# Four attention layers on one core: row maxima formed for two batches at once with GpSimd, weights three batches behind, norms moved to ScalarE

## The chip, the cores and the metric

The kernel runs on one core of a Trainium2 chip. The metric is the device time of one execution in microseconds. An engine is named as in the profile: PE (TensorE, its weight loads are PEld), DVE (VectorE), ACT (ScalarE), POOL (GpSimd), SP (SyncE, here only an issuer of DMAs).

## What is computed

A residual stream `x` of 32 batches x 128 tokens x 128 features goes through four pairs of a gated attention and a gated feed-forward part. Cut to what matters here:

```python
x = x + tanh(g_xattn[0]) * attn0(x, ctx)     # 16 heads of 8, keys from the context, masked
x = x + tanh(g_ffn[0])   * ffn0(x)           # dense, ternary weights, 128 -> 512 -> 512 -> 512 -> 128
x = x + tanh(g_xattn[1]) * attn1(x, ctx)     # 16 heads of 8, keys from the context and from x
u = mla_attention(norm(x))                   # causal, 16 heads of 4; then 8 experts, the best 2
x = x + tanh(g_ffn[1])   * (u + experts1)
x = x + tanh(g_xattn[2]) * attn2(x, ctx)     # 8 heads of 16, masked
x = x + tanh(g_ffn[2])   * (norm(x) + experts2)
x = x + tanh(g_xattn[3]) * depool(x, ctx)
x = x + tanh(g_ffn[3])   * quantised_ffn(x)  # int8-like activations: round(v * 127 / max|v|), clipped
```

Each attention is `softmax(q k^T) v` over 128 queries and 128 or 256 keys.

## The kernel before, in words

**A planner and five programs.** `make_plan` (line 491) writes out by hand one list of steps. `reckon` (line 97) gives each kind of step its cost per engine in nanoseconds and `LANDING` the time of its DMAs; `Plan.do` keeps a clock for each engine with them. Work that is not in the main loop (norms, transposes, splits, loads, expert blocks) waits in the list `side` and is put between main steps by `run_side`, `fill` and `flush`, as the planner's clocks say that its inputs are there. Then `tensor_program`, `vector_program`, `scalar_program`, `pool_program` and `sync_program` walk the same list, and each issues what is its own. So every engine's queue is in order, all waits are semaphore counts, and a cost in `reckon` changes no instruction but can change the order of all of them.

**An attention** (`attention`, line 730) works on batches in 32 time steps plus a `lag`. In step t it makes the scores of batch t (`s_unit`) and the weights of batch t - lag (`st_unit`). Scores are queries x keys into PSUM on PE; DVE reduces them over the keys to negated row maxima `mneg` (`scores`, line 2052). The weights need the transposed scores (keys x queries) less the maximum: PE computes them again the other way round over 99 rows instead of 96, where rows 96 to 98 of the tile `Q8` hold the maximum in three bf16 parts, and ACT takes the exponential out of PSUM (line 2428). PE then multiplies them with the values (`sums`).

**The maxima's way** (`max_parts`, `m_turn`): when the last scores of a batch are reduced, DVE makes the three bf16 parts with four small instructions (lines 2061 to 2064), PE transposes them (line 1722), ACT copies them to `mT` (line 2419), and SP stores them into `Q8` with three DMAs, for each batch. `lag` is 2 for 16 heads and 4 for 8 heads. The weights of a batch wait for these DMAs (`maxima`).

**Rows of the heads.** Queries and keys are split into bf16 parts (`split`, on POOL or DVE), stored to scratch memory in HBM (`parts_store`, three DMAs for a destination) and loaded back in the layout of the heads (`rows_load`: 384 KB a tile for 8-wide heads). Tiles hold three pairs of batches. The loads of pair p are issued at the end of time step `load_step[p] = max(2 * (p - A.R) + 1 + lag, 2 * p - 4)`, where `A.R` is 3 for 16 heads, and its scores start in step 2p.

**Norms**: DVE takes the statistics (`norm_in`, lines 2003 and 2006), POOL the reciprocal root (lines 2642 to 2659), DVE writes the result (`norm_out`, lines 2025 to 2029). **Experts**: blocks of 256 sorted tokens; for the first experts ACT does the tanh, DVE the gate (lines 2257, 2259) and the copy of the output out of PSUM (`block_down`, line 2265). POOL scatters the tokens (line 2622) and fetches the results (line 2628) with indirect DMAs. **The quantised part**: DVE scales and rounds in two instructions (2357, 2358: adding a large constant rounds) and clips, ACT takes the constant off (2539); for the hidden layer ACT scales (2551), DVE rounds and clips (2380), POOL takes the constant off (2677).

The stages by time in the profile: first attention 43 to 330 us, dense part 330 to 631, second attention 631 to 987, causal attention with the expert front beside it 987 to 1367, rest of the first blocks to 1535, third attention with blocks and fetches 1535 to 1790, second experts, depool and quantised part 1790 to 2425.

## Time and profile before

| | |
|---|---|
| median of 3 runs | 2424.68 us (2423.02 to 2434.64) |
| the profiled execution | 2426.92 us |
| its span, first to last instruction | 2425.1 us |
| PE busy | 1735.3 us, 72% |
| DVE busy | 1436.1 us, 59% |
| ACT busy | 918.9 us, 38% |
| POOL busy | 702.1 us, 29% |
| mean granted TensorE clock | 0.811 |

The span is the trace's; the 1.8 us around it belong to the execution. The engines' busy times overlap, and none fills the span, so the table alone does not name a bound; the waits inside a stage do. In the timeline a number in brackets is the idle time of the engine ahead of the instruction and what ended it.

### The profile page before, as it was taken

What the parts mean: (1) busy time and instruction counts of PE and PEld (TensorE: products, weight loads), DVE (VectorE), ACT (ScalarE), POOL (GpSimd) and SP (SyncE); (2) the same over time, 40 slices, a digit from 0 to 9 for tenths busy, and PEclk for the clock granted to TensorE, in tenths of its full rate; (3) what the DMA queues carried; (4) which work ended last, traced back from release to release, by engine and by line L of the source; (5) the groups of instructions that cost most, each with busy time, mean ns of one, the idle gap of its engine ahead of it and who ended that gap; (6) DMA issues with size and microseconds to landing.
All of it is one profiled execution on the core that took longest, in us unless ns stands there. A gap on an engine that the chain in (4) does not pass through costs nothing. (4 is left out here: it accounts for less than half of the span.)

```text
span 2425.1 us, 42255 instructions
## 1 busy us (share of the span) xinstructions
PE 1735.3 (72%) x14902; PEld 1225.0 (51%) x14902; DVE 1436.1 (59%) x4230; ACT 918.9 (38%) x1768; POOL 702.1 (29%) x1027
## 2 busy tenths in 40 slices
PE   2667879999688898898888875664661497874423
PEld 1344447677476666554545663553341486763212
DVE  5566655543476766567666556554774523648666
ACT  2334443333155555443333432231330264653223
POOL 3322100100331222124433116215426402151653
PEclk9878779999788888899888896796675698986555
DMA  6535546300155554321221112634520222120100
GB/s 174 117 82 107 113 125 213 70 1 1 35 98 94 107 94 78 97 48 48 55 50 48 43 64 63 138 95 140 116 63 29 77 71 66 58 68 22 42 27 9
DMA packets 189756, 184.46 MB, mean 76 GB/s; under 512 B 29508, under 2 KB 177924, under 8 KB 183556
## 3 DMA queue, kind: packets, MB, share of 16 engines
q1 hardware_dynamic: 180540, 145.04, 25.8%
q10 hardware_dynamic: 816, 19.92, 2.7%
q0 software_dynamic: 8192, 16.79, 2.4%
q8 instruction: 122, 2.00, 0.4%
q14 instruction: 86, 0.70, 0.1%
HBM read 119.47 MB, written 80.74 MB: 83 GB/s over the span
## 5 line engine op out<-in xcount | busy, mean ns | idle before, releaser
L2052 DVE TENSOR_REDUCE mneg<-psb 128x4 f32<-128x512 f32 (+1 forms) x576 | 387.5, 684 | 207.6 <-PE psb L1671 173.2
L2428 ACT ACTIVATE HB<-psb 128x512 f32<-128x512 f32 x384 | 222.3, 596 | 253.2 <-PE psb L1671 234.6
L1671 PE MATMUL psb<-K,Q 96*128 96x128 bf16 x1280 | 189.3, 251 | 54.0 <-DMA Q<-sc_q 32.1
L1671 PE MATMUL psb<-Q,K 99*128 99x128 bf16 x1280 | 147.9, 247 | 110.1 <-DMA Q<-mT 108.4
L2428 ACT ACTIVATE HB<-psb,bias 128x512 f32<-128x512 f32 x192 | 131.7, 686 | 227.5 <-PE psb L1671 201.7
L2646 POOL TENSOR_SCALAR rs<-mv 128x2 f32<-128x2 f32 (+1 forms) x96 | 22.3, 232 | 658.2 <-DVE mv L2006 650.3
L1671 PEld LDWEIGHTS psb<-Q,K 99*128 99x128 bf16 x1280 | 110.4, 113 | 146.0 <-issue 131.2
L1671 PEld LDWEIGHTS psb<-K,Q 96*128 96x128 bf16 x1280 | 112.1, 111 | 112.0 <-issue 54.0
L1671 PE MATMUL psb<-HB,VA 128*9 128x128 f32 (+1 forms) x2560 | 148.7, 311 | 27.3 <-ACT OE L2433 27.0
L1671 PE MATMUL psb<-K 128*128 128x256 f32 x576 | 155.6, 417 | 3.4 <-issue 1.5
L1671 PE MATMUL psb<-KS,Q 96*128 96x128 bf16 x1024 | 151.1, 238 | 9.2 <-DVE mneg L2052 8.3
L1671 PEld LDWEIGHTS psb<-K 128*128 128x128 f32 x576 | 114.2, 209 | 22.6 <-issue 6.1
L1671 PE MATMUL psb<-HB,VS 128*9 128x128 f32 (+1 forms) x2048 | 111.2, 293 | 2.3 <-issue 2.3
L1671 PE MATMUL psb<-Q,KS 99*128 99x128 bf16 x1024 | 109.5, 234 | 3.3 <-DMA Q<-mT 3.2
L1671 PE MATMUL psb<-cnegb,identb 128*128 128x512 bf16 x256 | 109.2, 427 | 0.5 <-issue 0.5
L1671 PEld LDWEIGHTS psb<-KS,Q 96*128 96x128 bf16 x1024 | 91.8, 106 | 27.8 <-DVE mneg L2052 12.0
L1671 PE MATMUL psb<-WB,HB 128*128 x768 | 98.2, 281 | 9.8 <-issue 7.4
L1683 PE MATMUL psb<-cst,OE 128*128 128x128 f32 x480 | 95.4, 325 | 13.4 <-issue 5.8
L1671 PEld LDWEIGHTS psb<-WB,HB 128*128 128x128 f32 x768 | 97.2, 198 | 13.1 <-issue 10.3
L2270 DVE TENSOR_TENSOR K<-psb,HB 128x256 f32<-128x256 f32 x48 | 20.4, 425 | 137.9 <-PE psb L1671 105.4
L1671 PE MATMUL psb<-biasT,selbb 96*128 96x512 bf16 x192 | 92.7, 483 | 1.0 <-issue 1.0
L1671 PEld LDWEIGHTS psb<-Q,KS 99*128 99x128 bf16 x1024 | 78.6, 105 | 23.2 <-issue 11.0
(433 smaller groups left out, 4031.8 us busy)
## 6 DMA issues: line engine op xcount, KB each, us to landing
tok_rows<-in_zero ACTq DMA_DIRECT2D x16, 1152.0 KB, 30.9
K<-sc_k SPq DMA_DIRECT2D x32, 384.0 KB, 4.9
Q<-sc_q SPq DMA_DIRECT2D x32, 384.0 KB
sc_q<-comp SPq DMA_DIRECT2D x48, 192.0 KB
K<-tok_rows SPq DMA_DIRECT2D x72, 128.0 KB
y_rows<-K SPq DMA_DIRECT2D x72, 128.0 KB
sc_q<-comp SPq DMA_DIRECT2D x48, 128.0 KB
vraw<-in_ctx SPq DMA_DIRECT2D x48, 128.0 KB, 7.0
```

Source lines behind the costliest of these rows:

```text
L1671: return pe.e.matmul(out, w, x, start=start, stop=stop, skip_group_check=True)
L1683: t = pe.e.transpose(o[:, 128 * j:128 * j + 128], src[:, 128 * j:128 * j + 128], ident)
L2052: t = e.tensor_reduce(m.mneg[:, s.b % 4, s.i * A.per:(s.i + 1) * A.per], PSB[s.use.bank].rearrange("p (h k) -> p h k", h=A.per), AX.X, ALU ...
L2270: v.done(e.tensor_tensor(y2, o2, m.b2bc[:, bass.ds(at_, 128)].unsqueeze(1).broadcast_to([128, 2, 128]), ALU.add), s.use.drained)
L2428: a.done(act(m.HB[:, s.slot, :], PSB[s.use.bank], ACT.Exp, bias=bz), s.use.drained)
L2646: then(e.tensor_scalar(r0, var, EPS, None, ALU.add))
```

## The change

- **Maxima.** DVE's four instructions a batch go. Once for two batches PE transposes `mneg` in fp32 (two instructions, into 16 or 8 rows x 256), ACT copies the result twice (to `m32` in fp32, to `mT` in bf16), POOL makes the second and third part with three instructions, and SP stores both batches with three DMAs (`max_store`).
- **Lag.** `lag` for 16 heads is 3 instead of 2. By the formula of `load_step` the row loads of pair p are then issued at the end of step 2p - 2 instead of 2p - 3. The weights of both batches of a pair wait for the one store.
- **Norms.** In the four attentions `norm_out` of the queries' input is ACT's (scale and bias); POOL makes the bias -mean * rstd with two instructions more, except in the causal attention, where the input is scaled only.
- **First experts.** `block_down` with its factor 2 is ACT's.
- **Rounding.** `quant_in` multiplies and adds the constant in four instructions of 128 columns; `quant_int` is POOL's and clips; the hidden layer's scaling by ACT goes, DVE scales and rounds in one, POOL clips and takes off the constant.
- **Planner.** The costs of SP's steps go from 100 to 250 up to 350 to 1500 for a destination or load; new kinds get costs. A copy of the values may be placed earlier (`copied`).
- **Constants.** Three constant blocks used only at the start lie in `U`, so the constants come in two DMAs.

```diff
-        self.lag = 2 if H == 16 else 4
+        self.lag = 3 if H == 16 else 4
...
-        "parts_store": lambda: (("sp", 250 * len(s.dests)),),
-        "rows_load": lambda: (("sp", 100),),
+        "parts_store": lambda: (("sp", 1500 * len(s.dests)),),
+        "rows_load": lambda: (("sp", 1100 if A.dh == 16 else 600),),
...
-        "max_parts": lambda: (("dve", 1050),),
-        "max_rows": lambda: (("pe", 130), ("act", 290), ("sp", 250)),
+        "max_rows": lambda: (("pe", 240), ("act", 760), ("pool", 2000)),
+        "max_store": lambda: (("sp", 1800),),
...
-            if i == n_s - 1:
-                k = b % 4
-                flush(("m", b - 4))
-                t = inc("dve", "max_parts")
-                do("max_parts", A=A, b=b, k=k, need=u.drained, free=mcb_free[k], done=t)
-                soon(lambda: m_turn(b, t), t, 0, ("m", b), m_turn)
+            if i == n_s - 1 and b % 2:
+                soon(lambda: m_turn(p, u.drained), u.drained, 0, ("m", p), m_turn)
+        def m_turn(p, t):
+            flush(("m", p - 1))
+            u = use(misc(), "act")
+            parts = inc("pool", "max_parts")
+            do("max_rows", A=A, p=p, need=t, use=u, free=(m32_free[0], mT_free[p % 2]), cst=t_cst, done=parts)
+            mneg_free[p % 2] = u.full
+            m32_free[0] = parts
+            soon(lambda: m_store(p, parts), parts, 0, ("m", p), m_store)
+        def m_store(p, parts):
+            do("max_store", A=A, p=p, need=parts, rows=prepped[p]["qk"])
+            mT_free[p % 2] = ready_m[p] = dma(f"dma_m{p % 2}", 3)
...
+        for b2 in range(2):
+            t = pe.e.transpose(PSB[s.use.bank][0:s.A.H, 128 * b2:128 * b2 + 128], m.mneg[:, 2 * (s.p % 2) + b2, 0:s.A.H], C("ident"))
...
+        act(m.m32[0:H, :], PSB[s.use.bank][0:H, 0:256], ACT.Copy)
+        a.done(act(m.mT[0:H, s.p % 2, 0, :], PSB[s.use.bank][0:H, 0:256], ACT.Copy), s.use.drained)
...
+        x, parts = m.m32[0:H, :], m.mT[0:H, s.p % 2]
+        g.wait_ge(before[0], s.use.drained)
+        step(e.tensor_tensor(x, x, parts[:, 0, :], ALU.subtract))
+        g.wait_ge(before[0])
+        step(e.tensor_copy(parts[:, 1, :], x))
+        g.wait_ge(before[0])
+        done(e.tensor_tensor(parts[:, 2, :], x, parts[:, 1, :], ALU.subtract), s.done)
...
+            then(e.tensor_tensor(mean, mean, r1, ALU.mult))
+            done(e.tensor_scalar(mean, mean, -1.0, None, ALU.mult), s.rstd)
...
-        v.wait_ge(v.step(e.tensor_tensor(b4(xf), b4(xf), Sc[:, :, 0:1].broadcast_to([128, 4, 128]), ALU.mult)))
-        v.done(e.tensor_scalar(xf, xf, MAGIC, MAGIC + 127.0, ALU.add, ALU.min), s.done)
+        for j in range(4):
+            t = e.tensor_scalar(b4(xf)[:, j, :], b4(xf)[:, j, :], Sc[:, j, 0:1], MAGIC, ALU.mult, ALU.add)
+        v.done(t, s.done)
...
-        v.done(e.tensor_scalar(m.H[s.k][s.j], m.H[s.k][s.j], MAGIC, MAGIC + 127.0, ALU.add, ALU.min), s.rounded)
+        v.done(e.tensor_scalar(m.H[s.k][s.j], m.H[s.k][s.j], m.sc[:, s.k, s.j, 4:5], MAGIC, ALU.mult, ALU.add), s.rounded)
...
+        done(e.tensor_scalar(m.qn[s.k], m.xf3[s.k], MAGIC + 127.0, -MAGIC, ALU.min, ALU.add), s.done)
```

## Rows read from the trace of the kernel before

**Rows 1.** Windows by stage: busy us (x instructions) of each engine, PEclk, DMA share, GB/s.
```profile
core 0: us, PE busy (x) PEld busy (x) DVE busy (x) ACT busy (x) POOL busy (x), PEclk, DMA share, GB/s
43.00:330.00 287.00, 207.27 (x2273) 124.55 (x2270) 183.15 (x495) 109.03 (x198) 58.03 (x87) 0.82 0.46 93
...
631.00:987.00 356.00, 297.62 (x4255) 229.50 (x4254) 246.53 (x606) 188.97 (x392) 94.81 (x168) 0.84 0.48 89
987.00:1367.00 380.00, 324.83 (x3088) 197.65 (x3084) 242.36 (x816) 145.24 (x316) 123.03 (x220) 0.87 0.21 56
...
1535.00:1790.00 255.00, 171.67 (x1393) 120.29 (x1393) 161.99 (x525) 82.49 (x174) 89.69 (x140) 0.74 0.47 117
1790.00:2425.00 635.00, 338.57 (x2105) 268.71 (x2105) 358.21 (x1189) 225.66 (x447) 231.83 (x286) 0.70 0.15 45
```

**Rows 2.** Who waited for mT (us, times): first, second, causal attention, in this order.
```profile
  PE psb L1671: 64.1, 15
...
  PE psb L1671: 41.2, 13
...
  PE psb L1671: 4.5, 3
```

**Rows 3.** Timeline, one pair of batches in the first attention: start, us, engine, instruction [idle].
```profile
193.76 1.53 SPq L2687 DMA_DIRECT2D sc_k<-comp  x3
...
196.62 0.32 SPq L2687 DMA_DIRECT2D K<-sc_k  x1
196.86 0.26 ACT L2419 ACTIVATE mT<-psb 48x128 bf16<-48x128 bf16 x1
...
197.92 1.77 SPq L2687 DMA_DIRECT2D Q<-mT  x3
...
200.58 0.31 DVE L2061 CAST mcb<-mneg 128x16 bf16<-128x16 f32 x1
...
205.53 0.58 PE L1671 MATMUL psb<-Q,K 99*128 99x128 bf16 x4 [4.60 <-DMA Q<-mT]
...
219.52 0.31 DVE L2061 CAST mcb<-mneg 128x16 bf16<-128x16 f32 x1
```

**Rows 4.** Windows inside that pair, columns as in rows 1.
```profile
206.00:213.00 7.00, 7.00 (x62) 4.17 (x64) 3.22 (x9) 2.82 (x5) 0.00 (x0) 0.51 0.38 107
```

**Rows 5.** Timeline, second attention: row loads, the store of maxima behind them, PE's wait.
```profile
766.84 0.33 SPq L2687 DMA_DIRECT2D K<-sc_k  x1
...
769.77 1.79 SPq L2687 DMA_DIRECT2D Q<-mT  x3
...
778.25 0.38 PE L1671 MATMUL psb<-Q,K 99*128 99x128 bf16 x4 [2.61 <-DMA Q<-mT]
```

**Rows 6.** Timeline of POOL in the causal attention: first and last of 8 scatters.
```profile
1201.05 1.12 POOL L2622 DMA_INDIRECT tok_rows<-HB,pidx  x1 [0.19 <-issue]
...
1210.05 0.96 POOL L2622 DMA_INDIRECT tok_rows<-HB,pidx  x1 [0.30 <-issue]
```

**Rows 7.** Timeline, first attention: the first of five POOL clears, a cast of DVE beside them.
```profile
110.70 3.51 POOL L2578 MEMSET KS<- 96x4096 bf16 x1
...
118.18 3.32 DVE L2063 CAST mcb<-mres 128x16 bf16<-128x16 f32 x1
```

**Rows 8.** Windows of the tile mcb alone, summed over the four attentions.
```profile
sum 1278.00, PE 32.18 PEld 12.97 DVE 109.47; mean PE 8.05 PEld 3.24 DVE 27.37
```

**Rows 9.** Groups by line and form: out<-in xcount | busy us, mean ns | idle before, releaser.
```profile
L2673 POOL TENSOR_TENSOR comp<-r,comp 128x256 bf16<-128x256 f32 x80 | 54.5, 681 | 6.4
...
L2677 POOL TENSOR_SCALAR Q<-Q 128x512 bf16<-128x512 f32 x16 | 24.2, 1512 | 8.4 <-DVE Q L2380 7.2
...
L2029 DVE TENSOR_SCALAR xn<-X,mv,rs 128x128 f32<-128x128 f32 x96 | 32.5, 408 | 4.4 <-POOL rs L2648 4.2
L1683 PE MATMUL psb<-cst,xn 128*128 128x128 f32 x128 | 32.1, 340 | 39.4 <-DVE xn L2029 28.9 <-issue 10.0 <-ACT mT L2419 0.5
...
L2551 ACT ACTIVATE Q<-Q,sc 128x512 f32<-128x512 f32 x32 | 20.5, 711 | 14.7 <-DVE sc L2374 14.7
...
L2414 ACT ACTIVATE xT<-psb 128x256 f32<-128x256 f32 x48 | 18.2, 382 | 59.6 <-PE psb L1683 52.7 <-remote 6.8
```

More of the change, by code:

```diff
@@ L157, in reckon @@
         "block_gate": lambda: (("dve", 1400),),
-        "block_down": lambda: (("pe", 900 if s.i == 0 else 1800), ("dve", 450)),
+        "block_down": lambda: (("pe", 900 if s.i == 0 else 1800), ("act", 480) if s.i == 0 else ("dve", 450)),
         "fetch": lambda: (("pool", 2550),),
@@ L458, in C @@
         o, w = CST[name]
-        return self.cst[:, o:o + w]
+        if o < CST["cneg"][0]:
+            return self.cst[:, o:o + w]
+        o -= CST["cneg"][0]
+        return self.U[:, :, :].rearrange("p b d -> p (b d)")[:, o:o + w]
     def col(self, name, i=0):
@@ L673, in norm_in, with norm_out @@
         return s
[L675 to L677 removed]
+    def norm_out(s, dst, free=None, done="normed", second=None, by="dve"):
+        t = inc(by, f"{done}_{by}")
+        do("norm_out", norm=s, dst=dst, free=free, done=t, second=second, by=by)
         return t
@@ L1946, in run_program, with norm_source, norm_views @@
             part(s)
+def norm_source(m, what, j):
+    name, i = what
+    if name in ("X", "U"):
+        return (m.X if name == "X" else m.U)[:, i + j, :]
+    if name == "CX":
+        return m.CX[:, j, 0:128]
+    return b4(m.xf3[i])[:, j, :]
+def norm_views(m, s, j):
+    name, i = s.dst
+    src = norm_source(m, s.second[0] if s.second else s.norm.src, j)
+    o = slice(128 * j, 128 * j + 128)
+    if name == "xn_heads":
+        return m.xn[:, i, o].rearrange("p (d h) -> p h d", h=16), src.rearrange("p (h d) -> p h d", h=16)
+    if name == "U":
+        return m.U[:, i + j, :], src
+    return (m.xn[:, i, o] if name == "xn" else m.nf[:, o] if name == "nf" else m.xf3[i][:, o] if name == "xf3"
+            else m.UP[:, o] if name == "UP" else x_front(m, s.dst)[:, o]), src
 def vector_program(v, plan, m, cu):
@@ L1989, in setup @@
             t = v.done(e.tensor_copy(m.biasT[:, i, :], PSB[7].bitcast(BF16)[0:96, 128 * i:128 * i + 128]), u.drained)
-    def source(what, j):
-        name, i = what
-        if name in ("X", "U"):
-            return (m.X if name == "X" else m.U)[:, i + j, :]
-        if name == "CX":
-            return m.CX[:, j, 0:128]
-        return b4(m.xf3[i])[:, j, :]
     def norm_in(s):
@@ L2009, in norm_out @@
     def norm_out(s):
-        nm, (name, i) = s.norm, s.dst
+        if s.by != "dve":
+            return
+        nm = s.norm
         v.wait_ge(nm.rstd, s.free)
@@ L2408, in setup, with norm_out @@
             a.done(t, ("clear_act", i + 1))
+    def norm_out(s):
+        if s.by != "act":
+            return
+        nm = s.norm
+        a.wait_ge(nm.rstd, s.free)
+        if s.second:
+            a.wait_ge(s.second[1])
+        for j in range(nm.n):
+            dst, src = norm_views(m, s, j)
+            if s.second:
+                t = act(dst, src, ACT.Copy, scale=m.rs[:, nm.k, j, 0:1])
+            else:
+                t = act(dst, src, ACT.Identity, bias=m.mv[:, nm.k, j, 0:1], scale=m.rs[:, nm.k, j, 1:2])
+        a.done(t, s.done)
     def transpose_x(s):
@@ L2515, in block_up, with block_down @@
             a.done(t, u.drained)
+    def block_down(s):
+        if s.i == 0:
+            a.wait_ge(s.use.full, s.free)
+            a.done(act(m.buf[0][s.h].ys[s.j % 3], PSB[s.use.bank][:, 0:256], ACT.Copy, scale=2.0), s.use.drained)
     def k8_ones(s):
@@ L2647, in norm_in @@
         if not s.twice:
-            done(e.tensor_tensor(r1, r0, power, ALU.pow), s.rstd)
+            if s.by == "act":
+                then(e.tensor_tensor(r1, r0, power, ALU.pow))
+                shift()
+            else:
+                done(e.tensor_tensor(r1, r0, power, ALU.pow), s.rstd)
             return
@@ L2697, in cst_load @@
     def cst_load(s):
-        load("cst", m.cst[:, :], io["cst"])
+        n, w = CST["cneg"][0], sum(w for _, w in CST.values())
+        load("cst", m.cst[:, :], io["cst"][:, 0:n])
+        load("cst", m.U[:, :, :].rearrange("p b d -> p (b d)")[:, 0:w - n], io["cst"][:, n:w])
     def ints_load(s):
```

171 lines of the change are left out of this document (74 added, 97 removed).

## The prediction

> **What bounds the kernel now.** I began with the windows by stage [rows 1]. PE is busy for 72%, 84% and 85% of the first, second and causal attention, at a granted clock of 0.82 to 0.87; behind 1790 us no engine is over 57%, so that stage is a chain of latencies. A busy PE at a low clock is not a PE at its peak, so I asked who waits. In the trace of the tile `mT` PE waits 64.1 us in the first attention, 41.2 us in the second and only 4.5 us in the causal one [rows 2]. The timeline of one pair shows the kind of wait [rows 3]: ACT has the maxima at 197.12 us, SP is just issuing row loads, stores at 197.92 to 199.69, and PE goes on at 205.53, 5.8 us after the last store was issued and after 4.60 us idle. The second attention repeats it: row loads from 766.84, the store at 769.77 to 771.56, PE idle for 2.61 us to 778.25 [rows 5]. Each costs twice: in the 7.0 us behind the wait PE is busy 7.00 us at a granted clock of 0.51, its lower level (1.2 of 2.4 GHz) [rows 4]. At the upper one this would be some 3.6 us, so 3.4 us more are lost. The pair takes 219.52 - 200.58 = 18.9 us; without wait and low clock it would be 18.9 - 4.6 - 3.4 = 10.9 us, some 5.5 us a batch.
>
> **The change, part by part.**
>
> **Maxima, first attention.** Removed: DVE's four instructions a batch, 109.5 us in all four attentions, 0.86 us a batch [rows 8]. DVE is busy for 64% there [rows 1] and PE sets the pace, so this buys nothing by itself. The new chain, from the last reduction of a pair: two fp32 transposes, no dearer than the 0.34 us of a full one [rows 9], 0.7 us; two ACT copies at 0.38, 0.8; three POOL instructions at most at 0.68, 2.0; three DMA issues 1.8 [rows 3]; landing. The landing is bounded by 1.3 us (a key store's last issue ends at 195.29, the load that waits for it goes at 196.62) and 5.8 us (behind row loads) [rows 3]. I take 2, near the first, because the store is now planned about 4.5 us into a step and the row loads at its end, so it goes ahead of them. With some 0.8 us (my estimate) for finishing what ACT, PE and POOL have in hand the chain is 8.1 us (7.4 to 11.9). It is covered by one batch: both batches of a pair wait for one store, and the first is due one whole step after the last reduction, as before. In the first attention 5.5 us cover it, so 2.6 us of wait stay in each pair, with a low clock behind about half of them, 1.7 us. The stage's mean pair is 287 / 16 = 17.9 us [rows 1], the new one 10.9 + 2.6 + 1.7 = 15.2, plus 1 us for row loads (below): 16.2 us, and 16 x 1.7 = 27 us are won. The five POOL clears at 110.7 to 126.2 us [rows 7] stand in the maxima's way once, some 7 us. **-20 us** (-70 to +20).
>
> **Lag and row loads.** They now have one step to land instead of two. From 766.84 to 778.25, 11.4 us, everything issued there had landed, maxima last [rows 5]; the rows alone must be earlier. The second attention's step without wait would be 356 / 32 - (2.6 + 3.4) / 2 = 8.1 us [rows 1, 4, 5]. So I allow 1 us a pair in both attentions; the ends are 0 and 3.3 us, 11.4 less 8.1.
>
> **Maxima, second attention.** The chain of 8.1 us meets a cover of 8.1 us: the wait goes. A pair is now 22.3 us, then 16.3 + 1 = 17.3, and 5 us a pair would be won. For a quarter of the pairs I keep the low clock, 0.9 us, and I add 1.2 us for the extra instructions of PE and ACT in front of their matmuls (two fp32 transposes and a norm on ACT, 0.34 to 0.4 us each [rows 9]). That leaves 2.9 us, x 16 = **-47 us** (-90 to 0).
>
> **Causal attention.** Almost no wait for maxima stands there [rows 2], so none can be won. DVE loses 0.86 us and half a norm of 2 x 0.41 us a batch [rows 8, 9], about 1.3 x 32 = 40 us of 242 busy [rows 1]; with PE busy 85% I count a quarter as time, -10. Against it stands POOL: eight scatters fill it from 1201.05 to 1211.01 us [rows 6]; a part of the maxima behind them is 10 us late with a cover of 11.9 us (380 / 32 [rows 1]) less the chain of 8.1. That is a wait of up to 6 us for each of the eight groups, if it falls so; I count one in six: +8. **-2 us** (-25 to +45).
>
> **Third attention.** There the lag is 4 and a pair has two steps of cover. POOL, busy 35% [rows 1], carries fetches; DVE, busy 64%, gets 40 us lighter. I let them cancel: **0 us** (-20 to +25). `block_down` costs ACT 0.38 us x 48 where ACT has room (32%): nothing; were it not hidden, 18 us.
>
> **Last stage.** In the chain of a group one ACT scaling of 0.71 us goes, four short DVE instructions take the place of two, and POOL's 1.51 us replace an ACT instruction of about 0.71 [rows 9]: 0.8 - 0.7, near zero, and DVE has less to wait for. I take **-3 us** (-20 to +15). SP issues 192 store DMAs fewer, 113 us of its queue at 0.59 us; it is waiting anyway outside the loads. The two DMAs of constants cost one issue, 0.5 us at most. The planner's new costs reorder all stages; what that does no row shows, and I allow it 20 us either way in the range.
>
> **Sum**: -20 - 47 - 2 + 0 - 3 = -72 us against the profiled execution's 2426.9 us: 2354.9. It lies 2.2 us above the median, so the forecast is 2353 us, -3.0%.
>
> **A rule against it.** While POOL clears, a cast of DVE takes 3.32 us [rows 7], where the mean of DVE's four instructions is 109.5 / 128 / 4 = 0.21 us [rows 8]. The Trainium skill (GPSIMD Engine Reference, Key points) says that GpSimd shares its SBUF interfaces with VectorE, and so instructions of the two can hold each other up. The trace agrees for clears. By it work sent to POOL would be partly paid for by DVE; this is the last rival.
>
> **Rivals.**
> 1. *Row loads take over.* One step of 5.5 to 8 us is too short, PE waits at the scores instead, and the clock falls as before. For it: 11.4 us from load to the end of what was issued [rows 5]. Against it: the maxima are now ahead of the loads, and a wait for them lengthens the very step that covers the loads. All of the gain in the first attention goes and 3.3 + 3.4 - 1 = 5.7 us a pair return in the second, more than its 2.9: that stage gains nothing; with -5 of the rest 2420, and 2386 if half the pairs are hit. I give 2410, chance 0.17.
> 2. *Slower: POOL's queue holds the maxima up.* Place: the three POOL instructions behind scatters, fetches, splits and clears. It decides from the point where the chain passes 8.1 us in the second and 11.9 us in the causal attention, so from 4 us of queue. Price: eight bursts of 6 + 3.4 us in the causal attention, 75 us, 25 us of the same in the third, 7 for the clears, against the 67 us of the first two and 3 of the last: 2424.7 + 107 - 70 = 2462; with two thirds of the bursts it is 2426, the point where nothing is left. I give 2445, chance 0.13.
> 3. *All waits go.* The planner fills the 2.6 us with side work, and the low clock goes with them. First attention 16 x (17.9 - 10.9 - 1) = 96 less 7 for the clears, second 16 x (5 - 1.2) = 61, rest -15: 2424.7 - 165 = 2260; with half of the further gain, 2306. Chance 0.13.
> 4. *DVE pays for POOL.* 64 x 2.0 us of maxima and 12 us of integers on POOL, 140 us; if a quarter of it holds DVE and half of that is time, 18 us: 2371. Chance 0.05, little else changed.
>
> The forecast has 0.52, with a range of its own of 2320 to 2390.
>
> **The numbers.** A measurement of this kernel can tell some 0.5%, 12 us, from no change. Faster: the forecast, rivals 3 and 4 and 0.07 of rival 1: 0.77. Same: the rest of rival 1 and a little of rival 2: 0.10. Slower: 0.13. The range 2285 to 2440 leaves out the far end of rival 3 and the worse half of rival 2.
>
> **What would show it.** The wait of PE for `mT` falls from 64 to about 40 us in the first attention and under 12 in the second; the second attention takes about 310 us, its clock above 0.92; the first about 267; the causal within 20 us of 380; the stage behind 1790 within 15 us of 635. PE waits for `Q<-sc_q` under 20 us in each. I am wrong if waits for rows stand where those for maxima stood, if POOL's parts come more than 4 us after ACT's copies, or if most of the gain lies in a stage with no wait for maxima.

## The result, and the profile after

The changed kernel takes 2456.73 us (median of 4, 2448.20 to 2465.92) beside 2424.89 us for the kernel before in the same comparison: ratio 1.0124, interval 1.0070 to 1.0177. It is slower by 1.2%, where I forecast 3.0% less time. The profiled execution took 2449.95 us with a span of 2448.1, 23.0 us more than before's span. DVE is busy for 1287.4 us, 149 less than before, and POOL for 863.5, 161 more: the work was moved as the diff says, and the time did not follow.

First the windows by stage, columns as in [rows 1]. The stages lie later than before, so the bounds are the changed kernel's own (first, second, causal and third attention, last stage).

```profile
43.00:350.00 307.00, 201.01 (x2297) 123.01 (x2295) 148.77 (x350) 124.90 (x229) 94.41 (x169) 0.82 0.45 91
638.00:1015.00 377.00, 296.68 (x4318) 228.99 (x4318) 215.68 (x458) 201.07 (x430) 135.28 (x247) 0.85 0.48 90
1015.00:1415.00 400.00, 325.28 (x3114) 199.61 (x3115) 215.84 (x661) 160.46 (x356) 155.87 (x279) 0.84 0.20 53
1583.00:1860.00 277.00, 172.85 (x1438) 118.18 (x1437) 151.42 (x456) 102.09 (x218) 142.42 (x236) 0.73 0.46 112
1860.00:2448.00 588.00, 320.35 (x2033) 258.82 (x2032) 333.05 (x1096) 198.40 (x399) 240.88 (x269) 0.72 0.16 47
```

The clocks of the first three attentions stand at 0.82, 0.85 and 0.84, where [rows 1] has 0.82, 0.84 and 0.87, and each of these windows is longer but the last. For a like-for-like account I cut every trace at the last exponential of ACT in each attention and in the dense part behind the first, and at the first reduction of the third attention. In us:

| trace | first att. | dense | second att. | causal att. | to the third | third att. | last | span |
|---|---|---|---|---|---|---|---|---|
| before | 338.6 | 264.8 | 395.7 | 389.1 | 144.9 | 266.8 | 625.3 | 2425.1 |
| after | 354.7 | 263.6 | 406.4 | 399.4 | 159.0 | 290.1 | 574.9 | 2448.1 |
| difference | +16.1 | -1.2 | +10.7 | +10.3 | +14.1 | +23.3 | -50.4 | +23.0 |

Each attention splits once more at its first exponential: its start is the time from the cut before it to its first exponential, its running part the rest. In us:

| trace | starts: first, second, causal | running parts: first, second, causal |
|---|---|---|
| before | 55.5, 47.4, 23.7 | 283.1, 348.3, 365.4 |
| after | 82.3, 72.4, 52.8 | 272.4, 334.0, 346.6 |

This is the reading that matters most. The three running parts got 44 us shorter, and the three starts 81 us longer.

The last two columns of the first table, third attention and last, belong together. On quiet executions (below) the changed kernel (after_again) has 1063 DVE instructions in its last stage, where the variant with before's maxima and the same rounding (a_oldmax2) has 1155: the longer third attention did work that otherwise comes behind it. Together the two stages win 27 us here, and 15.5 us on quiet executions.

Who waited, from the waits of PE by stage (us, times, longest). The first two lines are the first attention's, the last one is the causal attention's, those between are the second's:

```profile
PE psb L1686 <- DMA Q<-mT: 72.0, 15, 15.0
PE psb L1686 <- DMA Q<-sc_q: 33.0, 4, 14.4
...
PE psb L1737 <- DVE mneg L2076: 34.5, 13, 3.6
PE psb L1698 <- ACT xn L2435: 15.2, 2, 14.9
...
PE psb L1686 <- DMA KS<-sc_s: 10.4, 1, 10.4
...
PE psb L1686 <- DMA Q<-mT: 1.5, 2, 1.4
...
PE psb L1686 <- DMA Q<-mT: 18.7, 3, 12.6
```

The wait for maxima fell from 41.2 to 1.5 us in the second attention [rows 2], as forecast. In the first it rose from 64.1 to 72.0, in the causal one from 4.5 to 18.7. Of the 33.0 us for `sc_q`, 14.4 stand before the very first scores, where before has 18.3; 18.7 lie inside the attention. Two new kinds stand beside it: 34.5 us at L1737, PE's transposes of a pair's maxima waiting for DVE's last reduction, and single waits of 10 to 15 us where an attention starts.

Two neighbouring pairs in the first attention, from the timeline of the changed kernel, show how the chain of maxima behaves:

```profile
204.50 0.39 PE L1737 MATMUL psb<-cst,mneg 128*16 128x128 f32 x2
205.20 0.36 ACT L2448 ACTIVATE mT<-psb 16x256 bf16<-16x256 f32 x1
205.70 0.66 POOL L2700 TENSOR_TENSOR m<-m,mT 16x256 f32<-16x256 f32 x1 [3.29 <-ACT mT L2448]
207.58 1.77 SPq L2736 DMA_DIRECT2D Q<-mT  x3
209.45 0.52 SPq L2736 DMA_DIRECT2D K<-sc_k  x1
210.75 0.38 PE L1686 MATMUL psb<-Q,K 99*128 99x128 bf16 x4 [1.39 <-DMA Q<-mT]
...
218.07 0.39 PE L1737 MATMUL psb<-cst,mneg 128*16 128x128 f32 x2
218.78 0.36 ACT L2448 ACTIVATE mT<-psb 16x256 bf16<-16x256 f32 x1
219.14 0.22 POOL L2677 TENSOR_SCALAR rs<-mv 128x2 f32<-128x2 f32 x1 [4.40 <-DVE mv L2036]
...
220.86 0.67 POOL L2700 TENSOR_TENSOR m<-m,mT 16x256 f32<-16x256 f32 x1
222.13 0.32 SPq L2736 DMA_DIRECT2D K<-sc_k  x1
...
223.51 1.77 SPq L2736 DMA_DIRECT2D Q<-mT  x3
230.98 0.58 PE L1686 MATMUL psb<-Q,K 99*128 99x128 bf16 x4 [8.05 <-DMA Q<-mT]
```

In the upper pair POOL is free and starts 0.1 us after ACT's copy; the store goes ahead of the row loads; from the transposes to PE's matmul it is 6.3 us. In the lower pair POOL has four instructions of a norm first and begins at 220.86, 1.7 us after ACT was done. In SP's list the store stands behind the loads of rows there, and PE goes on 5.7 us after the last store was issued (223.51 + 1.77), against 1.4 us above. The chain is 12.9 us. Four of the 16 pairs show this, every second one from the seventh to the thirteenth, with waits of 7.5 to 8 us.

A fifth is the first pair of the attention: its store goes at 74.35 us, behind stores and row loads of a later pair, PE waits 15.0 us, and the first weights come at 82.3 us. The causal attention starts in the same way, with a wait of 12.6 us.

The start of the second attention, windows of before and of after (from the end of the dense part to the first weights, and from there to the last):

```profile
603.00:651.00 48.00, 34.24 (x170) 22.38 (x168) 22.59 (x42) 8.31 (x15) 21.02 (x12) 0.75 0.00 1
651.00:999.00 348.00, 298.31 (x4387) 230.34 (x4391) 234.72 (x590) 194.74 (x405) 80.27 (x158) 0.86 0.52 101
```

```profile
618.00:691.00 73.00, 40.61 (x217) 27.59 (x215) 21.13 (x44) 12.65 (x26) 31.22 (x35) 0.70 0.17 32
691.00:1024.00 333.00, 283.41 (x4330) 219.91 (x4327) 198.09 (x424) 200.44 (x426) 104.14 (x213) 0.90 0.52 103
```

The running part is 14 us shorter, at a clock of 0.90 in place of 0.86. The start is 25 us longer. So there is a gain from the waits removed, and more than it is spent before the first weights.

### The profile page after: what moved, and what is told of

Read it like the earlier page. It is cut to its first block and busy times, and to the rows that moved or that the text cites. A ratio compares the mean times of both kernels' runs of the same rounds, so it can differ in the third digit from the quotient of the medians.

```text
span 2448.1 us, 41731 instructions
## 1 busy us (share of the span) xinstructions
PE 1701.1 (69%) x14895; PEld 1209.6 (49%) x14902; DVE 1287.4 (53%) x3557; ACT 966.8 (39%) x1904; POOL 863.5 (35%) x1323
## 5 line engine op out<-in xcount | busy, mean ns | idle before, releaser
L1686 PE MATMUL psb<-KS,Q 96*128 96x128 bf16 x1024 | 153.5, 242 | 22.0 <-DVE mneg L2076 12.6
L1686 PE MATMUL psb<-HB,VA 128*9 128x128 f32 (+1 forms) x2560 | 151.1, 312 | 19.1 <-ACT OE L2462 10.4
L2700 POOL TENSOR_TENSOR m<-m,mT 16x256 f32<-16x256 f32 (+1 forms) x64 | 42.4, 663 | 337.6 <-ACT mT L2448 335.8
L1686 PE MATMUL psb<-Q,KS 99*128 99x128 bf16 x1024 | 108.2, 232 | 19.4 <-DMA Q<-mT 18.7
L1686 PEld LDWEIGHTS psb<-KS,Q 96*128 96x128 bf16 x1024 | 94.9, 109 | 45.1 <-issue 23.4
```

Source lines behind the costliest of these rows:

```text
L1686: return pe.e.matmul(out, w, x, start=start, stop=stop, skip_group_check=True)
L2700: step(e.tensor_tensor(x, x, parts[:, 0, :], ALU.subtract))
```

## The experiments

All ratios are against the kernel before, run in the same comparison. One thing must be known to read the stages: in four of the five comparisons the kernel before took 2343 to 2347 us, in one 2424 us, as in the first pair of traces. Most of the 80 us more lie behind 1000 us, and show as waits that no work of the kernel ends (last section). I call the two kinds quiet and held (held up by something unknown); stages behind 1000 us are compared inside one kind only. It is no property of a chip: the held comparison (a_ahead, c_mdve, b_scat1, o_roundold) and the quiet one with c_b3 were taken on the same one. Quiet stages:

| trace | first att. | second att. | causal att. | to the third | third att. | last |
|---|---|---|---|---|---|---|
| before_again | 336.1 | 388.8 | 358.8 | 129.5 | 253.1 | 608.7 |
| after_again | 351.3 | 408.4 | 378.0 | 138.0 | 288.7 | 557.6 |
| b_lag3 | 310.8 | 401.7 | 339.8 | 133.7 | 252.2 | 608.6 |
| a_oldmax2 | 323.0 | 393.0 | 328.0 | 140.7 | 262.8 | 599.5 |
| a_oldmax3 | 313.8 | 398.7 | 371.5 | 136.0 | 260.2 | 592.7 |
| a_first | 334.2 | 409.4 | 369.9 | 134.3 | 289.7 | 555.8 |
| a_mdve | 292.6 | 422.1 | 355.5 | 136.5 | 281.4 | 571.9 |
| c_om3 | 308.7 | 382.7 | 353.3 | 134.7 | 256.9 | 591.9 |
| c_b3 | 303.7 | 375.9 | 320.7 | 136.9 | 255.1 | 609.1 |

Starts and running parts of the three 16-head attentions in quiet traces:

| trace | starts: first, second, causal | running parts: first, second, causal |
|---|---|---|
| before_again | 55.9, 47.4, 23.6 | 280.2, 341.4, 335.2 |
| after_again | 80.7, 72.1, 54.8 | 270.6, 336.3, 323.2 |
| b_lag3 | 65.7, 75.4, 41.7 | 245.1, 326.3, 298.1 |
| a_oldmax3 | 66.2, 74.9, 42.0 | 247.6, 323.9, 329.5 |
| a_first | 68.6, 72.5, 42.1 | 265.6, 336.9, 327.7 |
| a_mdve | 68.7, 74.9, 45.1 | 223.9, 347.2, 310.4 |
| c_b3 | 59.2, 50.4, 24.6 | 244.5, 325.4, 296.1 |

**Lag and maxima apart.** Theory L: the third step of lag costs. Theory M: the pairwise maxima on GpSimd cost. Four kernels cross the two.

b_lag3:

```
-        self.lag = 2 if H == 16 else 4
+        self.lag = 3 if H == 16 else 4
```

> The kernel before with one number changed: weights come three batches behind the scores in the three attentions of 16 heads, not two. Theory L (the third step of lag): each of these attentions lasts one step more, and the maxima's cover grows by a step, so PE hardly waits for mT; but row loads have one step less. Net under L: +10 to +16 us in each of the three attentions in start-up and end, less what the removed waits give, so 2430 to 2470 us, with the first weights of the first attention at about 65 to 80 us in place of 55. Theory M (the maxima of a pair on GpSimd make the loss, lag is harmless): this kernel is as fast as before or faster, 2380 to 2425, since 64 + 41 us of waits for mT go.

Measured: 2318.55 us, ratio 0.988 (0.983 to 0.994). The two largest groups of score matmuls of its PE (busy us, mean ns | idle before, releasers) show why:

```profile
L1671 PE MATMUL psb<-K,Q 96*128 96x128 bf16 x1280 | 189.4, 251 | 142.6 <-DMA Q<-sc_q 62.8 <-DMA KS<-sc_s 38.0 <-DVE mneg L2052 30.7
...
L1671 PE MATMUL psb<-Q,K 99*128 99x128 bf16 x1280 | 143.8, 243 | 1.5 <-ACT HB L2428 0.8 <-DMA Q<-mT 0.7
```

The waits for maxima (111.0 us in before_again) are down to 0.7. Waits for rows took part of their place: 62.8 us for `sc_q` where 28.5 stood (18 us of both before the first scores), 38.0 for `sc_s`. The three starts are 56 us longer, the three running parts 87 us shorter. So a lag of three is a gain on before's own maxima, with longer starts and late rows as its price. Theory L is wrong on the sum for this kernel, though right that the starts cost. Of the causal attention's 19 us not all need be the lag's: the pause told of below is not in this trace either.

a_lag2 (the same line back to 2, on the changed kernel):

> The changed kernel with weights two batches behind again, the maxima still made for pairs. Now the even batch of a pair is due before the pair's odd scores have long been made, so the cover is none. Both theories expect it slower than the changed kernel: at some 5 to 8 us a pair for 48 pairs, 2600 us or more, less one step of lag in each attention. If it is within 20 us of 2457, the maxima's chain is covered by something else and the lag cost what it gave.

Measured: 2597.85 us, ratio 1.106 (1.100 to 1.112); PE waits 437.2 us for mT. Pairs need the third step. The two edits hang together.

a_oldmax3 (before's `max_parts`, `max_rows` and tiles put back into the changed kernel, with SP's part reckoned at 1800 ns where before has 250; the lag stays three):

```
-            if i == n_s - 1 and b % 2:
-                soon(lambda: m_turn(p, u.drained), u.drained, 0, ("m", p), m_turn)
+            if i == n_s - 1:
+                k = b % 4
+                flush(("m", b - 4))
+                t = inc("dve", "max_parts")
+                do("max_parts", A=A, b=b, k=k, need=u.drained, free=mcb_free[k], done=t)
+                soon(lambda: m_turn(b, t), t, 0, ("m", b), m_turn)
```

> The changed kernel with the maxima of before (one batch at a time, parts by DVE, four DVE instructions a batch) and the lag of three. Theory L: the loss stays, 2440 to 2470 us, the first attention ends within 8 us of 354.7. Theory M: the loss goes, 2400 to 2425, and PE's waits for mT fall from 129 us to under 30.

Measured: 2354.77 us, ratio 1.005 (1.002 to 1.008). The waits for mT are 2.6 us, and the first attention takes 313.8 us where the changed kernel takes 351.3. Against the changed kernel's 1.021 (next group) that is 1.6%: what the pairwise maxima on GpSimd cost at this lag. Its starts are those of b_lag3, 56 us over before's, so the other 24 of the changed kernel's 81 come with the new maxima.

a_oldmax2 (the same with a lag of two):

> The changed kernel with the maxima and the lag of before: what is left of the change are the norms on ScalarE, the new costs of SP's work for the planner, the shorter rounding and the first experts' rows on ScalarE. Theory L and theory M both: the start of each attention is as before, and the 50 us that the last stage wins stay, so 2375 to 2400 us. Theory C (the planner's new costs and the norms make the loss, not the maxima): about 2450, with the first attention's end still 10 us or more behind 338.6.

Measured: 2302.82 us, ratio 0.980 (0.975 to 0.985). The last stage is only 9 us shorter than before's, not 50, and with the longer third attention nothing is left of it. The gain is 13 us in the first attention and 31 in the causal one. With lag 3 the same rest of the change loses 32 us in the causal attention (371.5 against b_lag3's 339.8). Beside the rest of the change the third step of lag costs 2.5% (0.980 to 1.005), where on before it wins 1.2%; so of the 4.1% between a_oldmax2 and the changed kernel the lag has the larger part, and the maxima 1.6%. Neither theory L nor theory M is enough alone.

**Both kernels again, and the planner's costs.** before_again and after_again give quiet traces.

> The kernel before itself, for a trace on the chip on which the experiments run. All theories: the ratio is 1 within 0.3%, and the causal attention shows the pause of some 15 us in its score reductions, near the middle of the last third, that the trace of before has from 1255.7 to 1273.4 us.

Measured: ratio 1.000 (0.998 to 1.002), the pause as expected, from 1235.6 to 1254.7 us.

> The changed kernel itself, for a trace on this chip. All theories: 1.2% slower, ratio 1.007 to 1.018. Theory L+M (both the third step of lag and the pairwise maxima cost, the rest gives 2%): the loss against the variant with the maxima and the lag of before (0.98) is 3.3%, of which the lag is 2.5% and the maxima 0.8%, as the last runs had it.

Measured: 2393.19 us, ratio 1.021 (1.018 to 1.024), a little more than the 1.012 of the first comparison.

a_cost and b_cost (the eight SP costs of the other kernel; `rows_load`, for one, is 600 or 1100 in the changed kernel and 100 in before):

> The changed kernel, with the planner told the costs of SP's work (stores of parts, loads of rows, keys and values, zeroing, blocks) of the kernel before. It changes the written order only. Theory P (the loss comes from the order that the planner writes with the new costs): below 1.000, since the steps of the attentions lose nothing to SP. Theory L+M: 1.00 to 1.025, the waits of 8 us at every second pair of the first attention stay.

> The kernel before with the new planner costs of SP's work, nothing else. Theory P: slower, by 1 to 3%. Theory L+M: within 1% of before, on either side; the pause in the causal attention may go, which would give up to 0.8%.

Measured: 1.013 (1.010 to 1.016) for a_cost and 1.004 (1.002 to 1.005) for b_cost. The new costs lose 0.8% in the changed kernel by the ratios (0.5% by the medians) and 0.4% in before. They are a part of the loss, not its cause; both results lie outside what theory P expected.

**Why a chain of 8 us was not covered.** a_first:

```
                     if load_step[pp] == tstep:
+                        flush(("m", pp - 2))
                         loaded(pp)
```

> The changed kernel with one line more: a pair's store of maxima is written ahead of the row loads that come at the same step. Theory Q (SP's order: where the store goes behind the three loads of rows, PE waits 7 to 8 us at every second pair of the first attention; where it goes ahead, 1.4 us): the four waits of 7 to 8 us and some of the 12 to 15 us ones fall to under 4, the first attention's last weights come at 320 to 335 us in place of 351, and the whole is 10 to 30 us shorter, ratio 1.008 to 1.017 in place of 1.021. Theory R (the chain of pair's maxima is simply longer than the one step of cover, whatever the order): less than 5 us, and the rows are late instead.

Measured: 2359.46 us, ratio 1.008 (1.005 to 1.010): 1.3% from one line. The waits of 8 us at every second pair are gone; eight of 3.2 to 3.3 us stand in their place, one in each pair, and with those of the start it is 49.7 us in all (us, times, longest), where after_again has 70.6:

```profile
PE psb L1687 <- DMA Q<-mT: 49.7, 14, 13.1
```

In those eight pairs the chain is 8.05 to 8.15 us, though POOL still begins 1.9 to 2.0 us late, and the cover, the chain less the wait, is 4.9 us. The first attention takes 334.2 us in place of 351.3, but its running part is only 5 us shorter; 12 of the 17 us are the start, and the causal start is 12.7 us shorter too. The store of the first pair shows it, in after_again and then in a_first:

```profile
64.12 0.66 POOL L2704 TENSOR_TENSOR mT<-m,mT 16x256 bf16<-16x256 f32 x1
71.98 0.42 SPq L2736 DMA_DIRECT2D Q<-sc_q  x1
72.98 1.89 SPq L2736 DMA_DIRECT2D Q<-mT  x3
80.07 0.61 PE L1686 MATMUL psb<-Q,K 99*128 99x128 bf16 x4 [14.44 <-DMA Q<-mT]
```

```profile
64.12 0.66 POOL L2705 TENSOR_TENSOR mT<-m,mT 16x256 bf16<-16x256 f32 x1
64.81 1.88 SPq L2737 DMA_DIRECT2D Q<-mT  x3
68.00 0.61 PE L1687 MATMUL psb<-Q,K 99*128 99x128 bf16 x4 [2.37 <-DMA Q<-mT]
```

The parts are ready at 64.8 us in both. In after_again the store stands 8.2 us longer in SP's list, behind stores and loads of a later pair that are not ready themselves. The Trainium skill (DMA: Bandwidth & Descriptors, Queues, rings and completion order) says that an increment of a semaphore lands only after every earlier write from the same DMA engine. The trace agrees as far as it goes: 5.7 us behind the loads, 1.4 us ahead of them, for the same three small transfers; it does not show whether the data or the increment is what comes late.

a_mdve (POOL's `max_rows` becomes DVE's, and the planner reckons 900 ns on DVE for it where it had 2000 on POOL, so the written order changes too):

```
-            parts = inc("pool", "max_parts")
+            parts = inc("dve", "max_parts")
```

> The changed kernel with the three instructions that split a pair's maxima given to DVE in place of GpSimd; all else as in the changed kernel. Theory G (GpSimd's slow and late three instructions are what exceeds the cover): the chain gets 1.7 us in itself and up to 2 us of queue shorter, waits for mT fall from 152 us by 60 or more, ratio under 1.012. Theory Q: the order of SP decides, so less than half of that, unless the shorter chain lets the store pass the loads.

Measured: 2337.02 us, ratio 0.998 (0.995 to 1.000), 2.3% under the changed kernel. Its waits in the first attention, and one chain from its timeline:

```profile
PE psb L1686 <- DMA Q<-sc_q: 34.9, 4, 14.3
...
PE psb L1686 <- DMA Q<-mT: 10.1, 10, 2.1
```

```profile
173.10 0.38 PE L1737 MATMUL psb<-cst,mneg 128*16 128x128 f32 x2
...
174.19 0.41 DVE L2077 TENSOR_TENSOR m<-m,mT 16x256 f32<-16x256 f32 x1 [0.20 <-ACT mT L2456]
174.64 0.28 DVE L2078 CAST mT<-m 16x256 bf16<-16x256 f32 x1
174.95 0.41 DVE L2079 TENSOR_TENSOR mT<-m,mT 16x256 bf16<-16x256 f32 x1
175.39 1.78 SPq L2734 DMA_DIRECT2D Q<-mT  x3
177.82 0.32 SPq L2734 DMA_DIRECT2D K<-sc_k  x1
```

From the first of the three instructions to the store it is 1.20 us, on POOL it was 1.88 (205.70 to 207.58) and 2.65. Here the store stands ahead of the loads, and the first attention takes 292.6 us, 59 us less and the shortest of all, 47 of them in its running part. Its clock in the window from 43 to 293 us is 0.91, where after_again had 0.84. Theories G and Q both hold. What puts a store behind the loads is the written order, fixed before the run: in a_first POOL is as late and the store is ahead. a_mdve changes the engine and the order at once; beside a_first, whose order is right too, the engine is worth 8.1 us of chain against 5.5 and 3.2 us of wait a pair against 0.6 or none. The Trainium skill (GPSIMD Engine Reference, opening) calls GpSimd the wrong choice for ordinary elementwise work, VectorE being roughly twice as fast; here it is 0.66 us against 0.41. The queue on POOL cost more than that: of the 2.6 us of chain, 1.9 are the late begin and 0.7 the slower instructions. The clears are of this kind too, once: in after_again POOL begins the fourth pair's parts 11.8 us late, with a wait of 13.1 us behind it, and a_mdve has no such wait for maxima. At 0.998 a_mdve, with pairs, is 0.7% under a_oldmax3, without: forming maxima for pairs is no loss in itself.

**The start of an attention.** a_ahead:

```
-        load_step = {p: max(2 * (p - A.R) + 1 + lag, 2 * p - 4) for p in range(NP)}
+        load_step = {p: 2 * p - 4 if p < min(A.R, 2) else max(2 * (p - A.R) + 1 + lag, 2 * p - 4) for p in range(NP)}
```

A pair is loaded ahead of an attention where this step is negative. With a lag of two that holds for pairs 0 and 1 (-3, -1), with three for pair 0 alone (-2, 0).

> The changed kernel with two pairs of rows loaded ahead of each attention again. With a lag of three the rule for the step of a load leaves only the first pair ahead, with a lag of two it was two pairs; the slots are free either way. Theory A (the long start of the attentions, from the end of the stage before to the first weights 72 us in the second attention against 47 before, is that missing pair): the start gets 15 to 25 us shorter in the second attention and some 15 us in the first and the causal one, so 30 to 60 us in all, ratio 0.995 to 1.008. Theory L (the start is the one step more that the weights are behind, whatever is loaded): under 10 us in all, ratio 1.017 to 1.021.

Measured (held): 2407.43 us, ratio 0.993 (0.990 to 0.996), against 1.012 for the changed kernel in its own held comparison: 1.9%. From after's stages: first attention -17, second -10, causal -24 us; 42 of these 51 us are in the starts (68.6, 64.1 and 32.6 us). The timeline of the start of the second attention, in after and then in a_ahead:

```profile
660.18 0.69 PE L1698 MATMUL psb<-cst,xn 128*128 128x128 f32 x2 [14.94 <-ACT xn L2435]
680.54 0.26 PE L1686 MATMUL psb<-K,Q 96*128 96x128 bf16 x1 [10.41 <-DMA KS<-sc_s]
```

```profile
666.20 0.61 PE L1686 MATMUL psb<-Q,K 99*128 99x128 bf16 x4 [16.99 <-DMA Q<-mT]
```

Both waits went, one of 17 us for the first maxima came in place, and the first weights are 64 us behind the dense part, not 72. Theory A holds in the sum; in the second attention the start gets back 8 of its 25 us with GpSimd's maxima, where 15 to 25 were expected. In c_b3 (below) 618.6 - 568.2 = 50 us stand there, near before's 47, and its three starts together are 7 us over before's, where b_lag3's are 56.

**The pause in the causal attention.** In before_again DVE stands on one instruction of the first experts' table while the scatters land, and PE behind it (waits of DVE and of PE, 1230 to 1260 us):

```profile
DVE K L2213 <- DMA tok_rows<-HB,pidx: 10.8, 1, 10.8
```

```profile
PE psb L1670 <- DVE otmp L2076: 13.5, 1, 13.5
```

b_scat, everywhere, and b_scat1, in the causal attention alone:

```
-LANDING = {..., "scatter": 3500, ...}
+LANDING = {..., "scatter": 15000, ...}
```

> The kernel before with one number of the planner changed: it reckons 15 us in place of 3.5 for the landing of a scatter, so that the table of the first experts' blocks, whose DVE instruction stood 10.8 us for the scatters with all of DVE's queue behind it, is written later. Theory T (this one wait makes the pause in the causal attention and costs 25 to 30 us, and what the variants without it won was mostly this): ratio 0.986 to 0.990, no DVE wait for tok_rows over 2 us, the causal attention takes 330 us in place of 359. Against it: if the pause only moves elsewhere, the ratio is 0.997 to 1.003.

> The kernel before with 15 us reckoned for the landing of a scatter in the causal attention only (the run with it everywhere shortened that attention by 19 us and lost 50 us in the last stage, where fronts of the second experts waited for it in the written order). Theory T: the causal attention takes 330 to 342 us, the last stage is as before, ratio 0.988 to 0.996. If the pause's 19 us come back in the stage behind it, 0.998 to 1.002.

Measured: b_scat 2391.7 us, ratio 1.021 (1.017 to 1.025). The pause is gone and the causal attention takes 340.0 us, 19 less, but the last stage takes 50 us more: its fronts have scatters too. b_scat1 (held) gives 0.998 (0.996 to 1.001): causal attention -11 us, the stage behind it +16. Theory T falls. Removing a wait of 11 us by writing the table later moved its work to a stage with less to hide it under.

o_best1 (a_oldmax2, lag of three in the first attention alone, 15 us everywhere):

> The variant with before's maxima (0.980), with a lag of three in the first attention alone and the 15 us for the landing of a scatter. By the stages: the lag of three won 9 to 12 us in the first attention and cost 6 to 13 us in the second and the causal one. So about 10 us under that variant, ratio 0.972 to 0.978, if these effects add up; 0.980 or more if they do not.

Measured: ratio 1.001 (0.999 to 1.003). The 0.972 to 0.978 that was expected did not come. The third attention starts at 1432.0 us, 18 earlier than in a_oldmax2, and the last stage gives back 48: the same fault as b_scat.

**The rounding.** o_roundold (before's `quant_int`, `h_quant` and their ScalarE scaling put back into a_oldmax2):

> The variant with before's maxima and lag (0.980) with the rounding of before as well: ScalarE's scaling, then DVE. Theory F (the shorter rounding is what the last stage wins): third attention and last stage together 10 to 20 us longer than its 862 us, ratio 0.985 to 0.989. My sum of before the change had 3 us for it: 0.979 to 0.983.

Measured (held): 0.995 (0.993 to 0.997). As a ratio this cannot be set beside a_oldmax2's quiet 0.980. By stages, each against before in its own kind, the third attention and the last stage together are +1.0 us with the old rounding (893.1 against 892.1) and +0.5 us with the new (862.3 against 861.8). The rounding is worth nothing I can tell; theory F falls. What parts the two ratios lies in the causal attention, -6.5 us held and -30.8 quiet, where nothing is rounded.

**Together.** c_mdve (a_mdve, two pairs ahead, 15 us in the causal attention), c_om3 (a_oldmax3 with the same two), c_b3 (before with those two and the lag of three: three numbers and nothing else of the change).

> The changed kernel with the maxima's three instructions on DVE (0.998), two pairs of rows ahead, and 15 us reckoned for the landing of a scatter of the first experts alone. If theories A, G and T hold together: 0.998 less 1.5 to 2.5% for the start and 0.8 to 1.2% for the pause, 0.962 to 0.978. If A falls, 0.985 to 0.992; above 0.992 if T falls too.

Measured (held): 2373.08 us, ratio 0.980 (0.976 to 0.984), just outside the slow end of what was expected. It is 1.3% under a_ahead, with 42 us less in the first attention (295.0) and some lost again in the third and last.

> The changed kernel with the maxima of before (by batch, by DVE), the lag of three, two pairs of rows ahead, and 15 us reckoned for a scatter's landing in the causal attention. From the stages of the runs before: first attention 314 less 5 to 12 us for the pair ahead; second 398 less 20; causal 340 to 350 less 10; the rest as in the variant with before's maxima and lag. On a chip without the unexplained stops that is 2265 to 2290 us against 2344, ratio 0.966 to 0.977; on a chip with them, 0.975 to 0.988. If the pair ahead gives nothing here, 0.985 or more.

> The kernel before with those three numbers and nothing of the rest of the change: lag of three, two pairs ahead, 15 us for a scatter's landing in the causal attention. What it lacks against c_om3 are the norms on ScalarE, the new costs of SP's work, the shorter rounding and the first experts' rows on ScalarE. If that rest gives nothing, the two agree within 0.5%; by the first attention, where the variant with before's maxima and lag was 13 us ahead of before, c_om3 is 10 to 20 us faster.

Measured: c_om3 2296.61 us, ratio 0.980 (0.977 to 0.984), slower than its 0.966 to 0.977; c_b3 2274.48 us, ratio 0.970 (0.968 to 0.973). **c_b3 beats both kernels**: 3.0% under before. Against b_lag3 its starts are 49 us shorter, which is the rows loaded in time. Against before_again the first two attentions give 45 us and the causal one 38; the latter had only 5.5 us of waits for maxima, and the pause of DVE is absent from c_b3, so how much of the 38 the lag earned is not shown. The expectation that the rest of the change would give 10 to 20 us was wrong: it costs 22. The causal attention alone is 33 us longer, 353.3 against 320.7, and the third and last together win 15 of it back. The windows of that attention in c_om3 and in c_b3:

```profile
957.00:1309.00 352.00, 321.13 (x3027) 195.34 (x3015) 239.47 (x802) 155.21 (x347) 124.22 (x219) 0.88 0.21 51
```

```profile
944.00:1265.00 321.00, 300.42 (x3022) 182.98 (x3013) 244.32 (x836) 141.68 (x307) 123.35 (x219) 0.94 0.21 55
```

The number of matmuls is the same; in c_om3 PE waits 19.1 us in four times for `KS<-sc_f` and its clock is 0.88, not 0.94. With before's maxima this attention took 321 to 371 us in quiet traces, always for the same work.

## Why the prediction was wrong

**The step that failed first**: the sum has no term for the start of an attention. It priced a pair in the middle, 16 times, and put what comes before the first weights at nothing, without a reason. The running parts of the three 16-head attentions gained 44 us of the 69 that I forecast for them. Their starts cost 81 us: 56 by the lag (b_lag3, a_oldmax3), and 24 by the first pair's store, which is written behind stores and loads of a later pair (a_first takes them away). The rest is -1 us in the dense part, +14 on the way to the third attention and -27 behind it, together the +23 us measured.

**What bounds the kernel** held in part. PE waits for maxima in the first two attentions: b_lag3 took 111 us of waits down to 0.7 and won 1.2%, and c_b3 reached the 3.0% that I forecast for the whole change, though by before's maxima and not by pairs on GpSimd, and half of it in the causal attention, where I saw almost nothing to win. That the two figures agree is chance.

**Maxima, first attention** (-20 forecast, +16.1 measured: +26.8 in the start, -10.7 in the running part). In the running part, and for 12 us of the start, the step that failed is the landing: "I take 2, near the first, because the store is now planned about 4.5 us into a step and the row loads at its end, so it goes ahead of them." It does in 11 pairs of 16. In five it goes behind, the first pair among them, and up to 5.7 us came, the upper end I had myself read off [rows 3]. The chain was 6.3 and 12.9 us for 8.1; in a_first, with the order I had assumed, it is 8.1 us with a wait of 3.2 for my 2.6. So the sum of the links was sound and the order was not. The second mis-sized term is "some 0.8 us (my estimate) for finishing what ACT, PE and POOL have in hand": POOL alone was 1.7 us late. a_first took the order away, a_mdve both. The clears of [rows 7] are in it too, a wait of 12.84 us at 139.69 us where I had 7.

**Lag and row loads.** I charged 1 us a pair for the shorter time to land. What I did not see is that the rule for the load's step counts from the lag in the start-up too, so that one pair is ready where there were two. It is 56 us in the three starts of b_lag3 and 7 in those of c_b3, and 1.9% of the changed kernel (a_ahead). I quoted the formula and read it for a pair in the middle only.

**Maxima, second attention** (-47, +10.7). "The wait goes" was right, 41.2 to 1.5 us. The gain of the running part was 14 us, not 47, and the clock of the stage did not pass 0.92 but stayed at 0.85. In the wait's place come 34.5 us at PE's two transposes, which wait for a pair's last reduction at the head of PE's queue. I priced these instructions at their durations and left out what they wait for. The wait comes with the pairs and not with GpSimd: a_mdve has the same 34.5 us, and the runs with before's maxima at a lag of three do not have it. a_oldmax3 has 36.5 us of waits for the rows `sc_s` instead, and its running part is 12 us shorter. The start then cost 25.

**Causal attention** (-2, +10.3: +29.1 in the start, -18.8 in the running part). The bursts of rival 2 did not come: there are three waits for mT, 18.7 us, of which 12.6 is the start. In quiet traces with before's maxima this stage takes 321 to 371 us, starts of 24 to 42 us among it, by the written order; my 20 us either way for it was too little.

**Third attention and last stage** (-3, -27). My two windows, read singly, would have told a gain of 50 us, of which 23 come back as a longer third attention. **To the third**, +14.1 us held and +8.5 quiet, had no term in my sum and no run here explains it.

**Rivals.** Rival 2 had the right engine, POOL in front of the maxima, and the wrong stage and size: norms and clears in the first attention, not scatters in the causal one, and 1.7 us of queue behind a norm, under the 4 us from which it was to decide. Rival 1 was right in kind and too dear: in b_lag3 rows took over and it is still faster, and in the changed kernel they are 18.7 us inside the first attention, where I had allowed 20. Rival 3's premise, no wait for maxima at all, came true in b_lag3 and gave 1.2%, in c_b3 3.0%, not the 5 to 7% that I worked out. Waits for rows are a part of the difference, 62.5 us for `sc_q` in c_b3 where before_again has 28.5, and 21.0 for `sc_s`. Rival 4: DVE's 576 reductions took a mean of 684 ns before and 686 after, with 161 us more on POOL. These read PSUM; of the forms that both kernels have, some between SBUF tiles did grow (`U<-KS,gk,U` from 358 to 398 ns), but over all 3327 instructions of the forms that stand eight times or more in both it is 9.8 us. Little was paid.

**What stays open**: which edit of the rest (norms on ScalarE, the new costs, the first experts' rows) turns the causal attention from -31 us at a lag of two to +32 at three. Costs alone are 0.4 to 0.8%. Norms and rows were not tried alone, and neither were the two pairs ahead and the landing of the scatter apart in c_b3.

## What to carry to other kernels

Before a chain is said to be covered, write down for two neighbouring rounds what stands ahead of it in each queue, the DMA queue's own included: here a small store behind three loads landed 4 us later, one behind a later pair's whole preparation was issued 8 us later, and the engine that took over a link brought its own queue with it. When a pipeline is made deeper, price the start of each loop by the same formula as its middle: here the starts cost nearly twice what the middles gained. And where a stage gets faster, add the next one to it before believing the number.

## What the runs showed of the hardware that I had not expected

The same kernel on the same data took about 2345 us in four comparisons and 2424 us in two, with the first 1000 us alike (PE busy for 803.47 and 804.73 us at a clock of 0.88 and 0.89). In the held executions waits appear from about 1050 us on that the profile puts down to "remote" (nothing of this core). Each of the six held traces has 34 to 38 of them over 2 us on ACT and DVE; none of the 14 quiet traces has one behind 300 us. From the timeline of before, with all engines standing at once:

```profile
1673.38 0.38 ACT L2433 ACTIVATE OE<-psb 128x256 f32<-128x256 f32 x1 [12.62 <-remote]
1673.82 0.63 PE L1671 MATMUL psb<-HB,VA 128*17 128x128 f32 x8 [23.39 <-ACT OE L2433]
1674.13 0.69 DVE L2052 TENSOR_REDUCE mneg<-psb 128x4 f32<-128x512 f32 x1 [14.83 <-remote]
```

A wait that stands in every trace is no sign of it: PE's 9.83 us before 1913.58 us in before has its like in before_again too, 9.83 us before 1845.09. What holds the core is not shown; that an effect of 3.4% can sit in one comparison and not in the next is why every ratio here is against runs of before beside it.
